# Two attentions of a transformer block in equal beats, with packed causal tiles, halved value products and loads by batch

## The reference

```python
x = x + attn_a(layernorm(x))   # 16 heads of 8 features, causal, fp32 softmax
x = x + ffn(layernorm(x))      # silu gate, two 512x512 gelu layers, ternary weights
x = x + attn_b(layernorm(x))   # 16 heads of 8, rotary q and k, not causal
x = x + ffn(layernorm(x))      # the same weights again
```

## Time and profile before

| stretch (us of the span) | what | length | PE busy | DVE busy | ACT busy | POOL busy | clock |
|---|---|---|---|---|---|---|---|
| 19.57 to 757 | attention a | 737.43 | 619.35 | 501.02 | 431.89 | 362.26 | 0.93 |
| 757 to 1133 | ffn | 376.00 | 352.63 | 293.97 | 225.29 | 203.68 | 0.97 |
| 1133 to 2034 | attention b | 901.00 | 745.74 | 709.70 | 593.76 | 239.65 | 0.94 |
| 2034 to 2412.2 | ffn | 378.20 | 354.05 | 294.41 | 225.32 | 203.52 | 0.96 |

### The profile page before, as it was taken

The page is one execution under the profiler, slowest core; times in us unless marked ns, Lnnn a source line. Parts: engine busy times, 40 slices in busy tenths (PEclk is TensorE's granted clock), DMA queues, the critical chain, the costliest instruction groups (busy, mean ns, idle before and its releaser), DMA issues. The chain is left out here.

```text
span 2412.1 us, 36803 instructions
## 1 busy us (share of the span) xinstructions
PE 2071.8 (86%) x13122; PEld 960.1 (40%) x13122; DVE 1810.1 (75%) x2590; ACT 1476.3 (61%) x2980; POOL 1010.6 (42%) x1184
## 2 busy tenths in 40 slices
PE   1789999999884999997489898989889885899998
PEld 0223333333321777785112222222222212777776
DVE  5677777777642888883488889888898851888884
ACT  0166666666662666664047777777777774566665
POOL 2355555655431565654422332232322200456564
PEclk8699999999985999998569999999999997999999
DMA  5535454545310000000433344334343310000000
GB/s 153 118 78 107 85 108 89 105 91 105 73 22 11 1 1 1 1 1 27 95 64 64 77 82 88 70 64 89 82 82 64 63 20 12 5 14 14 11 12 18
DMA packets 99851, 136.45 MB, mean 57 GB/s; under 512 B 20560, under 2 KB 81488, under 8 KB 93520
## 3 DMA queue, kind: packets, MB, share of 16 engines
q1 hardware_dynamic: 99664, 134.02, 26.3%
HBM read 67.91 MB, written 55.57 MB: 51 GB/s over the span
## 5 line engine op out<-in xcount | busy, mean ns | idle before, releaser
L599 DVE TENSOR_REDUCE b_negmax<-ps_max 128x2 f32<-128x1024 f32 x512 | 613.8, 1220 | 92.4 <-PE ps_max L719 91.0
L685 ACT ACTIVATE b_prob<-ps_score 128x512 f32<-128x512 f32 x1024 | 545.8, 599 | 207.6 <-PE ps_score L704 206.4
L685 ACT ACTIVATE a_prob<-ps_score 128x512 f32<-128x512 f32 (+3 forms) x1024 | 383.7, 438 | 214.4 <-PE ps_score L704 212.9
L599 DVE TENSOR_REDUCE a_negmax<-ps_max 128x2 f32<-128x256 f32 (+3 forms) x512 | 403.1, 820 | 131.2 <-PE ps_max L729 121.3
L704 PE MATMUL ps_score<-b_stack_q,stack_k 50*128 50x512 bf16 x1024 | 259.1, 388 | 56.8 <-ACT b_prob L685 48.8
L746 PE MATMUL ps_out<-b_prob,b_v_aug 128*9 128x512 f32 x2048 | 268.6, 596 | 17.7 <-ACT b_o_raw L658 11.6
L516 POOL TENSOR_SCALAR_AFFINE_SELECT a_prob<-a_prob 128x512 f32<-128x512 f32 x256 | 161.9, 635 | 266.8 <-ACT a_prob L685 266.7
L719 PE MATMUL ps_max<-stack_k,b_stack_q 48*128 48x512 bf16 x1024 | 231.3, 397 | 25.9 <-DVE b_negmax L599 17.3
L1003 PE MATMUL ps_score<-fa_h,w_hi 128*128 128x512 f32 x1024 | 248.3, 397 | 0.7 <-ACT fa_h2f L946 0.4
L1003 PE MATMUL ps_score<-fb_h,w_hi 128*128 128x512 f32 x1024 | 247.6, 396 | 0.7 <-ACT fb_h2f L946 0.4
L704 PEld LDWEIGHTS ps_score<-b_stack_q,stack_k 50*128 50x128 bf16 x1024 | 63.9, 93 | 418.2 <-ACT b_prob L685 337.7
(11 more groups left out here) (139 smaller groups left out, 2962.3 us busy)
## 6 DMA issues: line engine op xcount, KB each, us to landing
stack_k<-d_stack SPq DMA_DIRECT2D x64, 384.0 KB, 5.6
d_stack<-a_parts SPq DMA_DIRECT2D x64, 192.0 KB, 2.8
a_stack_q<-d_stack SPq DMA_DIRECT2D x32, 384.0 KB, 5.4
d_stack<-b_parts SPq DMA_DIRECT2D x64, 192.0 KB, 2.8
b_stack_q<-d_stack SPq DMA_DIRECT2D x32, 384.0 KB, 5.4
d_stack<-a_parts SPq DMA_DIRECT2D x64, 128.0 KB, 2.8
d_stack<-b_parts SPq DMA_DIRECT2D x64, 128.0 KB, 2.8
d_stack<-a_parts SPq DMA_DIRECT2D x64, 64.0 KB, 2.5
```

The source lines that it names most:

```text
L599: last = dve.tensor_reduce(m["negmax"][:, t, :, p], dve_banks("max", k)[:, :, lo:hi], AX.X, ALU.max, negate=True)
L685: act.activation(m["prob"][u % PROBS][:, g, lo:S], act_bank("score", 4 * u + g)[:, 0:S - lo], ACT.Exp).then_inc(s["prob"], 1)
```

## The change

A step is cut into beats, 20 in attention a and 32 in attention b. Each beat has one pair of score banks of 512 columns, one row-maximum turn, and (at the beats that a table names) a block of value products. In the causal case a bank holds one key tile of 512 columns, or two tiles of 384 + 128 or 256 + 256 columns; the row-maximum turns hold 128 + 384, 512, or 256 of two pairs, the last reduced by one instruction. Value products are cut in two parts of the width. The mask that TensorE adds to the maxima is made of products with 64 rows each, two for each diagonal block of a head. The other work has new places (CAUSAL_AT, ROTARY_AT), separately for each engine, and TensorE's queue has no second score part in a beat: its order is maxima, scores, value products, other work (MSWX) in attention a and scores first (SMWX) in b.

The exponentials' buffers are 8 of 2 heads, the same bytes. x is loaded one sequence at a time, at most three ahead. VectorE waits for the stage's loads only at its first projection, for the bias rows at v. The ffn weights are rounded by ScalarE at the start of step 0, the rest is subtracted by GpSimd in steps 0 and 1, and its maxima are taken by VectorE at the ends of steps 3 to 7. The k stacks are set to one in steps -1 and 0, no more in the setup, and in step 0 SyncE stores k before it loads the q stack. The ffn stage is as before.

```diff
-PROBS = 4
+PROBS = 8
...
+W_LOW_AT = ((0, 19), (1, 13), (1, 5), (1, 5), (1, 5))
+X_AHEAD = 3
...
-            dve.memset(m["ps_out"][:], 0.0)
-            for c in range(STACKS):
-                last = dve.memset(m["stack_k"][c][:], 1.0)
-            last.then_inc(zeroed, 1)
+            dve.memset(m["ps_out"][:], 0.0).then_inc(zeroed, 1)
...
-            for lo, hi in ((0, 4), (4, 8), (8, 12), (12, 16)):
-                sp.dma_start(m["x"][:, lo:hi], a["x"][lo:hi].rearrange("b (t p) d -> p b t d", p=P))\
-                    .then_inc(loaded, 16)
-            sp.wait_ge(loaded, 64)
+            load_x(sp, m, a, 0)
+def load_x(sp, m, a, b):
+    wait(sp, m["x_in"][b % X_AHEAD], 16 * (b // X_AHEAD))
+    sp.dma_start(m["x"][:, b], a["x"][b].rearrange("(t p) d -> p t d", p=P)).then_inc(m["x_in"][b % X_AHEAD], 16)
...
+CAUSAL_AT = {"k": 3, "nm1": 1, "v": 5, "proj": 8, "xT": 9, "nm0": 13, "q": 13, "weigh": (4, 5, 6, 7, 7), "out": 8,
+             "P_nm1": 0, "P_rstd": 7, "P_v": 4, "P_bias": 11, "P_q1": 16, "P_q2": 17, "P_k1": 4, "P_k2": 8,
+             "P_nm0": 10, "P_o": 1, "D_stats": 6, "D_apply": 9, "D_q": 14, "D_k": 4, "D_v": 6, "D_inv": 12,
+             "D_proj": 9, "A_nm1": 2, "A_nm0": 14, "A_xT": 10, "order": "MSWX"}
+ROTARY_AT = {"k": 3, "nm1": 3, "kr": 6, "v": 15, "proj": 14, "xT": 19, "nm0": 23, "q": 23, "qr": 27,
+             "weigh": (4, 5, 6, 7, 8, 9, 10, 11), "out": 12, "P_nm1": 8, "P_rstd": 15, "P_v": 13, "P_bias": 15,
+             "P_q1": 24, "P_q2": 31, "P_k1": 11, "P_k2": 15, "P_nm0": 19, "P_o": 0, "D_stats": 16, "D_apply": 18,
+             "D_q": 24, "D_qr": 28, "D_k": 4, "D_kr": 7, "D_v": 16, "D_inv": 15, "D_proj": 15, "A_nm1": 4,
+             "A_nm0": 24, "A_xT": 20, "order": "SMWX"}
+class Plan:
+    def __init__(self, causal):
+        if causal:
+            per_group = [[(0, 0, 0, S)], [(1, 0, 0, S)],
+                         [(0, 1, 0, 3 * P), (0, 3, 3 * P, P)], [(1, 1, 0, 3 * P), (1, 3, 3 * P, P)],
+                         [(0, 2, 0, 2 * P), (1, 2, 2 * P, 2 * P)]]
+            diagonals = [(0,), (0,), (0, 3), (0, 3), (0, 2)]
+            products = [((0, 1), [(0, 0, S // 2, ((0, 0), (1, 0)))]),
+                        ((0, 1), [(0, S // 2, S // 2, ((0, S // 2), (1, S // 2)))]),
+                        ((2, 3), [(1, P, 3 * P, ((2, 0), (3, 0)))]),
+                        ((2, 3), [(3, 3 * P, P, ((2, 3 * P), (3, 3 * P)))]),
+                        ((4,), [(2, 2 * P, 2 * P, ((4, 0), (4, 2 * P)))])]
+            blocks = [(at, *what) for at, what in zip(CAUSAL_AT["weigh"], products)]
+            maxes = [[(0, 0, 0, P), (0, 2, P, 3 * P)], [(0, 3, 0, S)], [(0, 1, 0, 2 * P), (1, 1, 2 * P, 2 * P)],
+                     [(1, 0, 0, P), (1, 2, P, 3 * P)], [(1, 3, 0, S)]]
+            self.at = CAUSAL_AT
+        else:
+            per_group = [[(half, j, 0, S)] for j in range(T) for half in range(2)]
+            diagonals = [()] * len(per_group)
+            products = [((2 * j, 2 * j + 1), [(j, at, S // 2, ((2 * j, at), (2 * j + 1, at)))])
+                        for j in range(T) for at in (0, S // 2)]
+            blocks = [(at, *what) for at, what in zip(ROTARY_AT["weigh"], products)]
+            maxes = [[(half, t, 0, S)] for half in range(2) for t in range(T)]
+            self.at = ROTARY_AT
...
+            for i, name in enumerate(("bias_v", "bias_o")):
+                sp.dma_start(m["bias_row"][:, i, :], w[name].partition_broadcast(P)).then_inc(s["rows"], 16)
...
+                if n == 0:
+                    store(n, "stored_k", 1)
                 if on(n, 0):
                     load(n, "stack_q", "stored_q", 0)
+                if causal and on(n, -X_AHEAD):
+                    load_x(sp, m, a, n + X_AHEAD)
                 if on(n, 2):
                     aug(1, n - 2)
                 if on(n, 3):
                     numerators(n - 3)
-                if on(n, 0):
+                if n > 0 and on(n, 0):
                     store(n, "stored_k", 1)
                 if on(n, 3):
                     store_reciprocals(n - 3)
...
+            def mask(b, i):
+                pool.wait_ge(s["prob"], count(2 * BEATS, b, 2 * i + 2))
+                columns = prob(b, i).rearrange("p o (c k) -> p o c k", k=P)
+                if len(plan.diagonals[i]) == 2 and plan.diagonals[i][1] == 2:
+                    columns = prob(b, i).rearrange("p o (h c k) -> p (o h) c k", h=2, k=P)
+                    places = (0,)
+                else:
+                    places = plan.diagonals[i]
+                for c in places:
+                    tri = columns[:, :, c]
+                    last = pool.affine_select(out=tri, in_=tri, compare_op=ALU.is_ge, fill=0.0, base=0,
+                                              pattern=[[0, tri.shape[1]], [1, P]], channel_multiplier=-1)
+                last.then_inc(s["masked"], 1)
...
+            def low_of_weights(i):
+                _, name, cols = W_PIECES[i]
+                at = slice(W_AT[name], W_AT[name] + cols)
+                pool.wait_ge(s["w_hi"], len(W_PIECES))
+                pool.tensor_tensor(m["w_lo"][:, at], raw(i).rearrange("p k f -> p (k f)"),
+                                   m["w_hi"][:, at].bitcast(F32), ALU.subtract).then_inc(s["w_lo"], 1)
...
+            def rest_of_weights(i):
+                _, name, cols = W_PIECES[i]
+                at = slice(W_AT[name], W_AT[name] + cols)
+                dve.wait_ge(s["w_lo"], len(W_PIECES))
+                dve.tensor_reduce(m["w_rest"][:, i:i + 1], m["w_lo"][:, at].bitcast(F32), AX.X, ALU.max,
+                                  apply_absolute_value=True).then_inc(s["w_rest"], 1)
...
+                banks, pieces = dve_banks("max", i), plan.maxes[i]
+                (p, t, at, w), (p2, t2, _, _) = pieces[0], pieces[-1]
+                if p2 != p:
+                    last = dve.tensor_reduce(m["negmax"][:, t, :, p:p2 + 1], banks.rearrange("p o (c k) -> p o c k", k=w),
                                              AX.X, ALU.max, negate=True)
+                else:
+                    for _, t, at, w in pieces:
+                        last = dve.tensor_reduce(m["negmax"][:, t, :, p], banks[:, :, at:at + w],
+                                                 AX.X, ALU.max, negate=True)
...
+                    if causal and (n, i) in ((-1, AT["D_apply"] + 1), (0, AT["D_apply"] + 1), (0, AT["D_apply"] + 2)):
+                        c = n + 1 + i - AT["D_apply"] - 1
+                        dve.memset(m["stack_k"][c][:], 1.0).then_inc(s["cleared"], 1)
...
+                if causal and n == 0:
+                    act.wait_ge(s["w_raw"], 16 * len(W_PIECES))
+                    for i, (_, name, cols) in enumerate(W_PIECES):
+                        at = slice(W_AT[name], W_AT[name] + cols)
+                        act.activation(m["w_hi"][:, at], raw(i).rearrange("p k f -> p (k f)"), ACT.Copy)\
+                            .then_inc(s["w_hi"], 1)
...
+                    before, at = divmod(BEATS * b + i - PROBS, BEATS)
+                    if before >= 0:
+                        wait(act, s["pv"], count(BLOCKS, before, plan.block_of[at] + 1))
+                    for o in range(2):
+                        act.wait_ge(s["score"], count(2 * BEATS, b, 2 * i + o + 1))
+                        act.activation(prob(b, i)[:, o], act_bank("score", 2 * i + o), ACT.Exp).then_inc(s["prob"], 1)
...
+                pieces = plan.scores[i]
+                for piece, (p, j, at, w) in enumerate(pieces):
+                    for o in range(2):
+                        rows = slice(SIDE * o, SIDE * o + KROWS + AUG)
+                        if piece == 0:
+                            act_bank_free(pe, n, "score", 2 * i + o)
+                        mm = pe.matmul(act_bank("score", 2 * i + o)[:, at:at + w],
+                                       m["stack_k"][c][rows, p, P * j:P * (j + 1)], m["stack_q"][c][rows, p, S - w:S],
+                                       start=(piece == 0), stop=True, skip_group_check=(piece > 0))
+                        if piece == len(pieces) - 1:
+                            mm.then_inc(s["score"], 1)
...
+                    for half in range(2):
+                        for o in range(2):
+                            side = slice(SIDE * o, SIDE * (o + 1))
+                            at = ends[0] - P + SIDE * half
+                            if len(pieces) > 1:
+                                apart = ends[1] - ends[0]
+                                blocks = to[:, o].rearrange("p (c k) -> p c k", k=SIDE)
+                                diagonal = blocks[:, at // SIDE:(at + apart) // SIDE + 1:apart // SIDE]
+                                ident = m["ident_s"][side].rearrange("p (o c) -> p o c", o=1)\
+                                    .broadcast_to([SIDE, 2, SIDE])
+                            else:
+                                diagonal, ident = to[:, o, at:at + SIDE], m["ident_s"][side]
```

(64 more changed lines are left out.)

281 lines of the change are left out of this document (120 added, 161 removed).

## The result

| | before | after |
|---|---|---|
| median, us | 2416.9 (2413.4 to 2425.5, 4 runs) | 2231.2 (2230.4 to 2234.4, 4 runs) |
| span of the profiled execution | 2412.1 | 2232.4 |
| one step of attention a, mean of 12 | 39.55 | 33.71 |
| one step of attention b, mean of 12 | 49.46 | 47.61 |

The ratio is 0.9229, 95% interval 0.9203 to 0.9255. The forecast was 2217 with a range of 2155 to 2305.

A forecast was written before the change was run, and what follows sets the result against it. VectorE's work plus waits for TensorE's uneven queue was taken to bound the attentions. From 2413.8 us, -48 (b's steps), -108 (a's steps), -38 and -7.5 (their starts) and +5 (maxima of the weight rests) gave 2217, range 2155 to 2305.

The forecast's parts named there:

- Statement of the bound: Attentions: VectorE's work plus its waits for TensorE's uneven queue, 5.3 us a step in b, 7.1 in a.
- Steps of b: Attention b: a step falls from 49.5 to 46.5 us (44.8 to 49.5), -48 over 16 steps.
- 2.3 above VectorE's need: Attention b: slack left in the 46.5 us step over VectorE's 44.2, where today's is 5.3.
- rival 2: Both attentions: beats mesh, VectorE idles only 0.6 us a step; a at 31, b at 45, total 2164; chance 0.18.
- Steps of a: Attention a: a step falls to 32.8 us (30.5 to 39.5), 3.1 above a need of 29.7; -108 over 16 steps.
- the queues: SyncE's queue in a: k stack lands near 27 of 32.8 us, so the next step's first maxima don't wait.
- Masks of half rows: Attention a, TensorE: a pair of 64-row mask products takes 0.06 us, 40 pairs 2.4 us a step.
- rival 1: Both attentions: TensorE remains the bound, masks near their upper price; a at 36, b at 48.5, total 2300; chance 0.20.
- Start of a: Attention a's start: one load of x and short setup bring first scores near 67 us, -38 (-20 to -48).
- Start of b: Attention b's start: the rope table is waited for only at the first projection, -7.5 us (-4 to -11).
- only the starts: Whole kernel: steps stay at 39.5 and 49.5 us, only the starts gain, total 2373; chance 0.05.
- lockstep: Attentions: reduction and next product no longer overlap; b's step 59.9 us, a 39.4, total 2539, slower; chance 0.05.

The follow-up runs named there:

- Experiment 5: Changed kernel with attention b's value products over the whole width again, in beats 5, 7, 9 and 11: 2285.4 us, ratio 0.9464.
- experiment 9: Kernel of experiment 8 with the second half of the rows of maxima sent ahead of the numerators in a's SyncE queue: 2156.1 us, ratio 0.8919.
- experiment 1: Changed kernel with SyncE sending for the numerators (copies of ps_out) first in each step of attention a: 2206.1 us, ratio 0.9130.
- experiment 4: Changed kernel with attention a's masks of the maxima made again by one product on all 128 rows per head: 2265.8 us, ratio 0.9372.
- experiment 10: Kernel of experiment 9 with b's first value product of a group moved from beat 4 to 5, beside the second: 2171.9 us, ratio 0.8996.
- experiment 8: Changed kernel with the edits of experiment 1 and experiment 7, and k's lower parts in a moved from beat 8 to 6: 2173.0 us, ratio 0.8986.
- experiment 7: Changed kernel with GpSimd's k part and bias addition in attention b moved from beat 15 to 14, before VectorE normalises: 2202.0 us, ratio 0.9118.

## Why the prediction was right, and what it missed

- **Statement of the bound: right, shown in b.** Uneven pieces in TensorE's queue held VectorE up. Experiment 5 shows it directly: less work for TensorE in longer pieces costs 54 us and gives VectorE its old idle time back. In a only the masks and the start were undone, so that there the even beats are argued from the waits for maxima (7.5 to 2.7 us a step).
- **Steps of b, forecast 46.5, measured 47.61.** Between first and last score 41.1 us went where 48 were forecast. The term "2.3 above VectorE's need" had in it the waits for `ps_out`'s copy, which came (1.2 to 2 us a step were forecast; TensorE's weight loads waited 4.1 in two steps); what they cost by themselves is not shown. What the term lacked is that VectorE's need itself grows, by the two instructions held beside GpSimd (1.2 us a step), and the half clock behind them; and that VectorE would wait for the projections, 1.4 us a step. Without the first two the step is 45.5, nearer to rival 2 (45).
- **Steps of a, forecast 32.8, measured 33.71; first to last score 99.8 us less**, where the step term and the weight rests together gave 103. The needs of three engines were right: ScalarE 24.7 for 24, GpSimd 23.6 for 24, VectorE 30.3 for 29.6, where the excess is the held instruction (29.5 in experiment 9). TensorE's was put too high: in the undisturbed step its whole busy time, tails included, is 29.4, so the need lies below that and not at 29.7, still inside the bounds of 28 to 36. The step that failed is in **the queues**: I followed the loads of the stacks and left out the numerators, though their issues had moved behind the load of x and the step had become shorter. Experiments 1 and 9 price that order at 25 and 17 us, the second with the normalising of a moved away from GpSimd first.
- **Masks of half rows: right.** 0.07 and 0.12 us stand where 4 products of a beat were put at 0.12 (two pairs of 0.06). With the masks near their upper price rival 1 gave a step of 36; experiment 4, which pays the old price for whole masks, took 35.80, a kernel that rival 1 doesn't describe, so that the likeness is luck in part.
- **Start of a, forecast 38 less, measured 34.1** (71.5 for 67): the first statistics came at 4.1 us (6 to 8 forecast), the first maxima at 39.6 where about 35 were forecast, and 32 us later the scores, as forecast. **Start of b** 5.7 less (9.7 and 4.0 back) for 7.5. The ffn stages stayed: from the last addition to x of the attention before them to their own last, 378.0 us before and 378.1 after in the first, 375.9 and 377.2 in the second.
- **Rivals.** TensorE as the bound (2300), only the starts (2373) and lockstep (2539) did not come. Rival 2, 31 and 45 a step and 2164 in all, is what the kernel does once two queues and one collision are mended: 30.57, 45.51 and 2156. (Its "0.6 us a step" of idle time doesn't fit its own steps, which leave 1.4 and 0.8 above VectorE's need.) The forecast lay 14 us below the result, by luck in part: the two costs that I missed, 25 and 29 us alone and 75 with the rest of the reordering, stood against slack that I had put in partly without a mechanism for it (in a 3.1 us a step, carried over from b's 2.3).

The collision could have been read before. VectorE's row on the page of the kernel before:

```profile
L201 DVE TENSOR_SCALAR xhat<-x,mv,rstd 128x128 f32<-128x128 f32 x256 | 126.4, 555 | 62.8 <-POOL rstd L193 62.8
```

Its mean is 555 ns, while in a step of attention it was 339: in the ffn stages the same instruction was held, 28 of 64 of them in each, at 1.3 to 1.4 us beside a `tensor_tensor` of GpSimd. A deal of work that moves GpSimd's instructions against VectorE's had to be asked about it. The Trainium skill, SBUF — State Buffer, Who interferes with whom, states that a `tensor_scalar` can enter a mode in which it and GpSimd shut each other out for a whole instruction. The trace agrees: the two long ones end 0.08 us behind the cast and the `tensor_tensor` of GpSimd. The same section says that on trn2 a `tensor_reduce` never contends in this way, and the reductions beside GpSimd's work kept their 1.22 us.

## What to carry to other kernels

When a change makes a step shorter and adds issues to a queue, walk the whole queue again, for every transfer whose buffer the next step overwrites: the one left out sets the new step. Before removing a wait seen in the profile, count what its removal adds elsewhere (experiment 10 took away 1.2 us a step of TensorE's idle time, brought 1.9 of another wait and lost 16 us). When a mended cost brings nothing, look for the wait that took its place (experiment 8 in a, then experiment 9). Cutting long pieces so that every beat costs each engine about the same can pay even where it adds work to the engine that seemed the bound.

## What the runs showed of the hardware

- Four mask products of 64 rows (two halves of the rows, two outputs) take 0.07 us from start to start for 64 columns and 0.12 for 128; a pair on all 128 rows, which masks as much, takes 0.21 and 0.32 for 128 and 256 columns, with the matmuls around them in half rows, and the maxima before it 0.1 us more.
- A stretch of 3.3 us with TensorE busy for 1.76 was followed by 3.5 us at a granted clock of 0.55. So a stall of 1.5 us was paid for twice: with it gone (experiment 1) TensorE's busy time for the same work fell by 1.06 us a step in a. In b (experiment 7) the step fell by 2.1 us where VectorE got 1.2 back.
- VectorE's fp32 `tensor_scalar` from SBUF to SBUF was held until GpSimd's cast or `tensor_tensor` of 512 columns had ended: four took 2.32 us beside one of each, 1.11 without. Beside GpSimd's `tensor_tensor` of 32 columns one took 0.33 us, as alone, and the reductions from PSUM were not held by either.
